# Spikes of the q, k and v projections made on ScalarE as Relu of their signs instead of on VectorE

## What is computed

```python
x = x + _L0_conv_ref(_ln_c(x), ...)      # spherical transform, complex weights, inverse transform
t = t + _L0_ffn_ref(_ln_t(t))            # integer logic on 48 of the channels
x = x + _L1_conv_ref(_ln_c(x), ...)      # spiking attention
t = t + _L1_ffn_ref(_ln_t(t), ...)       # 8 experts, the best 2 of each token
```

```python
def step(v, xt):
    v = v + (xt - v) / TAU               # TAU = 2
    s = heaviside(v - v_th)              # 1 where v >= v_th
    v = v * (1.0 - s)                    # reset where it fired
    return (v, s)
q, k, v = (lif(bn(x @ lin_w[i].T + lin_b[i]), 1.0) for i in range(3))
o = lif((q @ k.T * SCALE) @ v, 0.5)      # 8 heads of 16 channels
return lif(bn(o @ lin_w[3].T + lin_b[3]), 1.0)
```

## Time and profile before

| | us |
|---|---|
| median of 3 runs | 1424.89 |
| the three runs | 1403.18, 1424.89, 1427.52 |
| the profiled execution | 1399.59 |
| its span, first to last instruction | 1397.8 |
| its mean granted PE clock, share of full speed | 0.844 |

### The profile page before, as it was taken

How to read it: one execution, slowest core, us unless ns; L and a number is a source line. 1 busy time by engine, 2 the same in 40 slices (tenths; PEclk the granted TensorE clock), 3 DMA queues, 4 the chain that set the end, 5 groups by cost and what they waited for, 6 DMA issues and landing times. The chain is left out here.

```text
span 1397.8 us, 23961 instructions
## 1 busy us (share of the span) xinstructions
PE 1031.5 (74%) x6628; PEld 879.5 (63%) x6629; DVE 856.6 (61%) x2741; ACT 655.3 (47%) x1400; POOL 573.8 (41%) x739
## 2 busy tenths in 40 slices
PE   7935997591166676867667744309999999999997
PEld 7824996371144554745546623308888888888886
DVE  5704441244455788898987575326666666666675
ACT  2424552221718688687776442114444444444443
POOL 2401000011101235667666566663555555555553
PEclk9976998796567788779879765559999999999999
DMA  9895982991001100100000000011111111111110
GB/s 281 146 200 99 205 173 74 236 231 45 20 20 34 33 20 25 32 19 15 25 17 25 25 20 21 32 56 31 42 40 46 46 46 46 46 46 48 45 41 6
DMA packets 124249, 93.08 MB, mean 67 GB/s; under 512 B 10632, under 2 KB 111348, under 8 KB 123921
## 3 DMA queue, kind: packets, MB, share of 16 engines
q1 hardware_dynamic: 115089, 74.87, 24.1%
q0 software_dynamic: 9088, 17.33, 3.8%
HBM read 55.61 MB, written 38.39 MB: 67 GB/s over the span
## 5 line engine op out<-in xcount | busy, mean ns | idle before, releaser
L1659 POOL DMA_INDIRECT out_dram<-res,index x156 | 155.9, 999 | 217.8 <-DVE res L1742 192.6
L1789 ACT ACTIVATE sil<-ps_h 128x512 f32<-128x512 f32 x156 | 93.2, 597 | 254.9 <-PE ps_h L1841 254.9
L1707 DVE TENSOR_TENSOR act_rows<-ps_h,sil 128x512 f32<-128x512 f32 x156 | 107.9, 692 | 133.4 <-ACT sil L1789 133.4
L1860 PE MATMUL ps_y<-r_raw,aT 128*128 x1248 | 164.8, 275 | 0.0
L153 POOL DMA_INDIRECT slots<-x_sb,r_pos x128 | 131.0, 1024 | 54.1 <-issue 33.0
L1860 PEld LDWEIGHTS ps_y<-r_raw,aT 128*128 128x128 f32 x1248 | 151.6, 192 | 0.1
L503 PE MATMUL ps_m<-wc,sblk 128*128 128x128 f32 x512 | 112.8, 397 | 38.2 <-ACT sblk L479 38.2
L1839 PE MATMUL ps_h<-wp,uTh 128*128 x312 | 137.6, 441 | 1.6 <-DVE uTl L1701 1.6
L503 PEld LDWEIGHTS ps_m<-wc,sblk 128*128 128x128 f32 x512 | 106.0, 212 | 45.1 <-issue 38.6
L1840 PE MATMUL ps_h<-wp,uTh 128*128 x312 | 124.7, 400 | 0.0
L1841 PE MATMUL ps_h<-wp,uTl 128*128 x312 | 123.1, 395 | 0.0
(11 more groups left out here) (233 smaller groups left out, 2472.1 us busy)
## 6 DMA issues: line engine op xcount, KB each, us to landing
slots<-zero SPq DMA_DIRECT2D x4, 2652.0 KB, 23.1
pay<-slots SPq DMA_DIRECT2D x39, 272.0 KB, 2.9
wc<-in_L_conv_w1r SPq DMA_DIRECT2D x8, 512.0 KB, 9.1
wc<-in_L_conv_w1i SPq DMA_DIRECT2D x8, 512.0 KB, 10.9
wc<-in_L_conv_w2r SPq DMA_DIRECT2D x8, 512.0 KB, 12.0
wc<-in_L_conv_w2i SPq DMA_DIRECT2D x8, 512.0 KB, 11.5
coefficients<-c SPq DMA_DIRECT2D x4, 1024.0 KB, 5.3
coefc<-coefficients SPq DMA_DIRECT2D x16, 256.0 KB, 7.9
```

The lines of the kernel that those rows point to most:

```text
L1659: nc.gpsimd.indirect_dma_start(out_rows, bass.IndirectOffsetOnAxis(at, 0), res[:, m % RES, :], None, bounds_check=TOKENS - 1, oob_is_err=F ...
L1707: nc.vector.tensor_tensor(act_rows[:, k], ps_h[:, k, :, DFF:], sil[:, k], ALU.mult).then_inc(s_act, 1)
L1789: nc.scalar.activation(sil[:, k], ps_h[:, k, :, 0:DFF], ACT.Silu).then_inc(s_sil, 1)
L1860: ins = nc.tensor.matmul(dst, aT[:, k, (2 * e + h) * P:(2 * e + h + 1) * P], raw[:, 4 + h, col], start=(h == 0), stop=(h == 1))
```

## The change

The spikes `spk` are no longer made by DVE. A new function on ACT, `spike_projected`, makes them as Relu of `sig_q`, in the queue behind `sig_q` and `sy` and ahead of everything in `behind`. DVE keeps the reset; its wait for `sig_q` now stands inside the branch for b < 7, so that in step 7 DVE has nothing to do with `sig_q` any more.

```diff
--- before.py
+++ after.py
@@ -1027,13 +1027,10 @@
 
         def projected(dve, w, b):
 
-            k = w * B + b
-            dve.wait_ge(s_sq, k + 1)
             if b < LAST:
+                dve.wait_ge(s_sq, w * B + b + 1)
                 state = ps_q[:, :, 0:3 * C]
                 nc.vector.scalar_tensor_tensor(state, sig_q[:, b % 2], 0.0, state, ALU.is_le, ALU.mult).then_inc(s_rq, 1)
-            need(dve, s_o, k - B + 1)
-            nc.vector.tensor_scalar(spk[:, b], sig_q[:, b % 2], 0.0, None, ALU.max).then_inc(s_spk, 1)
 
         def masked(dve, w, bp):
 
@@ -1290,6 +1287,14 @@
             act.wait_ge(s_qkv, k + 1)
             need(act, s_spk, k - 1)
             nc.scalar.activation(sig_q[:, b % 2], ps_q[:, :, 0:3 * C], ACT.Sign, bias=under_one[:, 0:1], scale=2.0 ** -b).then_inc(s_sq, 1)
+
+        def spike_projected(act, w, b):
+
+            k = w * B + b
+            act.wait_ge(s_sq, k + 1)
+            need(act, s_o, k - B + 1)
+            nc.scalar.activation(spk[:, b].rearrange("p j f -> p (j f)"), sig_q[:, b % 2].rearrange("p j f -> p (j f)"), ACT.Relu)\
+                .then_inc(s_spk, 1)
 
         def sign_attended(act, w, b):
 
@@ -1505,6 +1510,8 @@
                             sign_projected(act, i, b)
                         if k >= 1:
                             spike_output(act, *divmod(k - 1, B))
+                        if i < NP2:
+                            spike_projected(act, i, b)
                         behind(i, b)
                 sign_output(act, NP2 - 1, LAST)
                 spike_output(act, NP2 - 1, LAST)
```

## The result

The changed kernel takes 1425.3 us in the median of 20 runs (1414.7 to 1453.3 but for a single run of 2461.9), the kernel before 1414.2 us in the median of 20 (1394.2 to 1430.5). The ratio is **1.013, 95% interval 1.010 to 1.017**: slower by 1.3%. The ratio compares only the runs of the faster of two levels in which each kernel's times fall, 13 and 10 runs with medians of 1421.3 and 1403.3 us, so 18.0 us apart, while the medians of all runs are 11.1 us apart. Forecast were 12.2 us, 0.9%, and a time of 1437 us, which is 12 us too high, mostly because the three runs that it started from had a median of 1424.9 us and not 1414.2.

The account below looks back on a forecast made before the run. The stage was taken as bound by an exchange between DVE and ACT, in-order queues with little left. Window terms 0.6 + 2.3 + 4.2 + 4.4 + 0.7 gave +12.2 us on 1424.9: 1437 us, range 1402 to 1452.

Parts of the forecast that it names:

- Price: Each Relu on ACT: 844 ns, 0.74 us in the queue; each removed DVE instruction gives 0.27 us back.
- The release: Time from the end of sig_y or sig_q on ACT until the waiting DVE reset starts: taken as 0.10 us.
- the walk: Step-by-step tracing of delays through the engines' queues: window 4 ends 1.1 us later, all windows together +12.2 us.
- The section on what would show it: Expected signs in the profile, among them DVE busy down some 23 us and ACT up some 54.
- Step 1: Window 4: Relu pushes zT, u, x and the next sig_y by 0.74 us; +0.21 left after DVE's saving.
- Step 4: Window 4: r_y comes 0.95 us later, PE waits for it, so the next step's sig_q moves by 0.95.
- Step 5: Window 4: one Relu more ahead of r_y, next sig_q 1.69 us late; +1.13 for DVE's statistics and power.
- the Relu of step 6: Window 4: lies in ACT's 3.41 us wait for POOL before z.
- step 7's Relu: Window 4: pushes z, zT and PE's projection, which ACT's 3.21 us wait before power absorbs.
- A: Windows 3 to 6: DVE is the bound, ACT's waits take the Relu; together -9.6 us, 1415; chance 0.10.
- B: Whole kernel: gains and losses cancel through a short Relu or unseen slack; within 3 us of 1425; chance 0.17.
- C: Windows 3 to 6: ACT has no more lumps, all but two Relus on the path; +24.6 us, 1449.5; chance 0.10.

Follow-up runs that it names:

- mixed: Against the kernel before: Relu on ScalarE in steps 0 and 6 behind sy, in steps 4 and 5 last in the step; ratio 0.994, median 1398.4 us.

## Why the prediction was right, and what it missed

**Price.** The Relu at 844 ns, measured 837; in the queue 0.74 us, measured 0.74 (602.44 to 603.18 below). DVE's 0.27 us: 14.8 us in 64, 0.23 each. The release that was taken at 0.10 us takes 0.03 at most places, which moves the walk by less than 0.1 us. The section on what would show it spoke of 23 and 54 us of busy time; those were durations added up where neighbours overlap, and 14.8 and 46.2 is what a page shows.

ACT in window 4 of the kernel after, which answers the earlier trace rows:

```profile
595.53 0.22 ACT L1282 ACTIVATE power<-gap 128x16 f32<-128x16 f32 x1 [0.22 <-POOL gap L1180]
...
602.44 0.84 ACT L1296 ACTIVATE spk<-sig_q 128x768 bf16<-128x768 bf16 x1
603.18 0.58 ACT L1259 ACTIVATE zT<-ps_turn 128x512 f32<-128x512 f32 x1
...
626.37 1.64 ACT L1268 ACTIVATE r_y<-x_sb 128x128 f32<-128x128 f32 x4
...
630.75 0.90 ACT L1289 ACTIVATE sig_q<-ps_q,under_one 128x768 bf16<-128x768 f32 x1 [1.54 <-PE ps_q L1063]
...
632.58 1.64 ACT L1268 ACTIVATE r_y<-x_sb 128x128 f32<-128x128 f32 x4
...
640.01 0.90 ACT L1289 ACTIVATE sig_q<-ps_q,under_one 128x768 bf16<-128x768 f32 x1 [3.05 <-PE ps_q L1063]
...
641.11 0.83 ACT L1296 ACTIVATE spk<-sig_q 128x768 bf16<-128x768 bf16 x1
641.85 3.18 ACT L1251 ACTIVATE z<-x_sb,e_tmp 128x128 f32<-128x128 f32 x8
...
657.62 0.22 ACT L1282 ACTIVATE power<-gap 128x16 f32<-128x16 f32 x1 [1.91 <-POOL gap L1180]
```

**Walk through window 4.** Step 1: sig_q to sig_q 6.6 us instead of 5.9, as said. Step 4: r_y, then 1.54 us of wait for PE as before, and PE's own wait for r_y 2.75 instead of 2.40. Step 5: r_y stands one Relu later (632.58 follows 631.85 by 0.73), PE's wait is 2.65 instead of 1.92, both as forecast. Then the term that failed: **sig_q of step 6 was to be 0.74 us later from step 5 to 6, measured 9.3 - 5.9 = 3.4**. I had moved PE's instructions as rigid blocks; their durations doubled. In windows 3 and 6 the same step came out as forecast, 6.6 us, so this term failed in windows 2 and 4 and in part in 5. The wait before z, 3.41 us, into which the Relu of step 6 was to fall, is gone: the Relu at 641.11 is followed by z at 641.85 without idle time. The wait before power shrank from 3.21 to 1.91 us, absorbing step 7's Relu as said. The walk runs from one power to the next: window 4 took 62.1 us (595.53 to 657.62) instead of 56.6 (591.02 to 647.59), **+5.5 and not +1.1**; in the second profiles 62.1 and 57.2.

**The other windows**, start of sig_q to start of sig_q, means of the two profiles of each kernel, with the forecast in brackets: window 0 -2.8 (+0.6), 1 +2.1 (+2.3), 2 +6.9 (+4.2), 3 +1.9, 4 +4.6, 5 +1.7, 6 +4.1 (+1.1 each), 7 -1.2 (+0.7). Sum +17.3 against 12.2. (A single window can differ by 4 us between executions of one kernel, so these are signs, not proofs.)

From the first sig_q to the power of window 3 it is +6.2 us where the walk gave 7.1, from there to the power of window 7 +11.7 where it gave 4.4, and for the rest -0.6 where it gave +0.7. So it is the four windows with a power, 3 to 6, that were priced too low. In the mean of these four the signs were 0.3 us late at step 4 (walk 0.2), 1.2 at step 5 (0.95), 2.6 at step 6 (1.7), and the next power 2.9 (1.1). A third of the gap opens in the step from 5 to 6, where PE's level changed, and a half behind it, where the walk let DVE's slack and savings take 0.56 us off and 0.3 came on top. Why is not traced.

The granted clock does not explain the signs of all windows: it is higher after in window 0 (0.61 to 0.70), which got shorter, and in window 1 (0.77, then 0.83 and 0.86), which got longer, and lower in window 7 (0.73 to 0.70), which got shorter.

**Rivals.** A (DVE's saving counts) fell with the run without spikes: its cap was 24.1 us, the stage gave 1.6. B needed PE's waits for r_y to stay as they are; they grew by 8.1 us. C, the lumps used up, is partly what happened: the wait before z vanished in windows 2 and 4. With two Relus a step the waits before z and power fall to 3.8 and 4.2 us in all and the stage takes 513.6 us. The Trainium skill's rule (ScalarE: Activation LUTs, Rules for kernel authors: relu and max to VectorE) agrees in its direction with 837 against 363 ns; that a Relu is a plain loss is borne out here where no wait of ACT follows it, as in steps 1 and 2 (0.7 us each), while moving it in steps 0 and 6 cost nothing that could be measured.

**Sum.** The direction and the mechanism, work ahead of others in ACT's queue that DVE's saving does not repay, are shown by the runs without and with two Relus. The size was 12.2 us against 17.3 in the stage and 18.0 between the medians that the ratio compares; that the medians of all runs lie 11.1 apart is luck. The 5 us that are missing lie in windows 3 to 6. PE's lower level in the step from 5 to 6 is one part of them, and the walk had nothing for it; how much of the rest is the clock and how much the queue is not shown.

## What to carry to other kernels

An instruction moved to an engine with more idle time can be free only where one of that engine's waits follows it before anything that another engine waits for; read where it lands in each step of the loop, not the engine's busy share. Where the relieved engine waits for the loaded one, its saving is not a gain. And put such an instruction behind what others wait for, not ahead of it: the same 64 Relus cost 17.3 us of the stage ahead of the r_y, zT and z rows and 10.6 behind them, though this rests on one profile of the second and on ratios of 1.013 and 1.005 whose intervals overlap by 0.001; and four of eight in chosen places made the kernel 0.6% faster than before (interval 0.2 to 1.1%).

## What was not expected of the hardware

PE's granted clock in short stretches is either 1.00 or 0.50, and the same chain behind the same wait of 2.65 us got the one in windows 3 and 6 and the other in windows 2 and 4 of one kernel, in both of its profiles. Over kernels with the same PE instructions in the stage, PE's busy time went from 311.2 us (mixed) to 345.7 us (two Relus), its mean clock from 0.80 to 0.73, and one Relu more or less a window moved the stage by 10 to 15 us in single profiles. Both programs that were profiled twice gave the same stage within 0.8 us, so a pattern of levels can repeat from run to run. Filling a wait of PE with 16 useless matmuls of 128x128 brought the chain behind it from 5.28 to 2.75 us in window 2, changed nothing in windows 3 to 5, and in window 6 the chain took 4.25 us instead of 2.75. And in seven of the experiments an activation started up to 2.1 us after the matmul that it waited for, where 0.04 us is the rule.
